# Layer inputs and weights split on other engines, and a ring of four 512-column banks used as two slots of 1024

## What is computed

```python
# layer 0: one head of K0 = 32 channels, then a batch norm over all batches
q, k, v = Wq x + bq, Wk x + bk, Wv x + bv
x = batch_norm(gamma * (v softmax(q k)^T) + x)
# layer 1: group norm (32 groups), one head of 256 channels
q, k, v = split(qkv_w group_norm(x) + qkv_b)
x = x + proj_w (softmax(q k / 16) v) + proj_b
# layers 2 and 3: group norm, eight heads of 32 channels
q, k, v = split(qkv_w xn + qkv_b), per head
x = (xn in layer 2, x in layer 3) + proj_w concat(softmax(q k * 32 ** -0.5) v) + proj_b
```

## Time and profile before

| | us |
|---|---|
| median of 3 runs | 1860.53 (1860.29 to 1861.84) |
| the profiled execution | 1861.36 |
| its span, first to last instruction | 1859.6 |
| TensorE busy | 1673.1 (90%) |
| VectorE busy | 1048.1 (56%) |
| GpSimd busy | 1011.9 (54%) |
| ScalarE busy | 925.8 (50%) |
| mean granted TensorE clock | 0.941 |

### The profile page before, as it was taken

How to read it: one execution, slowest core, us unless ns; L and a number is a source line. 1 busy time by engine, 2 the same in 40 slices (tenths; PEclk the granted TensorE clock), 3 DMA queues, 4 the chain that set the end, 5 groups by cost and what they waited for, 6 DMA issues and landing times.

```text
span 1859.6 us, 25009 instructions
## 1 busy us (share of the span) xinstructions
PE 1673.1 (90%) x8222; PEld 1001.1 (54%) x8222; DVE 1048.1 (56%) x1635; ACT 925.8 (50%) x1487; POOL 1011.9 (54%) x402
## 2 busy tenths in 40 slices
PE   3888869999994789999999997999999999999987
PEld 2666747788883444545545544444454454455522
DVE  2445535454542466667567666675576576656611
ACT  2334414343331246665565564665666566556553
POOL 2323221211213148687677775787688678767764
PEclk7889979999997679999999998999999999999997
DMA  3000000000000330330330320303213123033000
GB/s 140 18 18 1 18 1 1 1 1 1 1 1 23 68 69 1 69 69 1 70 69 1 69 63 24 69 1 74 45 25 69 25 69 69 2 92 70 1 23 23
DMA packets 25000, 67.53 MB, mean 36 GB/s; under 512 B 7200, under 2 KB 8992, under 8 KB 24864
## 3 DMA queue, kind: packets, MB, share of 16 engines
q1 hardware_dynamic: 24864, 65.78, 14.5%
HBM read 7.82 MB, written 4.19 MB: 6 GB/s over the span
## 4 chain that ended last, share of the span: by engine, by line
PE 53%; ACT 4%; SPq 3%; issue 3%; DVE 2%; DMA 1%; POOL 1%; POOLq 0%; ACTq 0%; DVEq 0%
PE psA L952 15%; PE psO L871 12%; PE psD L927 12%; PE psD L79 10%; PE psO L874 4%; ACT PR L1127 3%; SPq L1213 2%; DVE BNS L1004 2%; SPq L1215 2%; DMA QS<-SL 1%; POOL PA L1193 1%; ACT XH L1071 0%; DMA QS<-MROW 0%; PE psD L922 0%; POOL SL L1173 0%
## 5 line engine op out<-in xcount | busy, mean ns | idle before, releaser
L1127 ACT ACTIVATE PR<-psA 128x512 f32<-128x512 f32 x1024 | 582.2, 597 | 480.8 <-PE psA L952 438.1
L1004 DVE TENSOR_REDUCE BNS<-psD 128x1 f32<-128x512 f32 x1024 | 633.5, 683 | 233.8 <-PE psD L927 233.7
L1193 POOL TENSOR_TENSOR PA<-PA,PR 128x2048 f32<-128x2048 f32 x128 | 585.6, 4575 | 16.4 <-ACT PR L1127 4.0
L952 PE MATMUL psA<-QS,KS 97*128 97x512 f32 x1024 | 461.1, 459 | 41.5 <-ACT PR L1127 33.6
L927 PE MATMUL psD<-KS,QS 96*128 96x512 f32 x1024 | 397.8, 429 | 23.4 <-DVE BNS L1004 11.3
L952 PEld LDWEIGHTS psA<-QS,KS 97*128 97x128 f32 x1024 | 191.4, 191 | 351.0 <-ACT PR L1127 199.2
L594 POOL TENSOR_SCALAR P<-P,RS 128x1024 f32<-128x1024 f32 x64 | 72.1, 1126 | 359.3 <-DVE RS L345 359.3
L871 PE MATMUL psO<-PR,V 128*32 128x512 f32 x2048 | 261.4, 618 | 0.7 <-ACT PR L1127 0.7
L927 PEld LDWEIGHTS psD<-KS,QS 96*128 96x128 f32 x1024 | 201.4, 197 | 82.0 <-DVE BNS L1004 37.1
L1193 POOL TENSOR_TENSOR PA<-PR 128x2048 f32<-128x2048 f32 x32 | 146.7, 4585 | 126.0 <-ACT PR L1127 126.0
L1173 POOL TENSOR_TENSOR SL<-SL,SH 128x1024 fp32r<-128x1024 f32 x34 | 80.6, 2373 | 155.2 <-ACT SH L1079 155.2
(11 more groups left out here) (131 smaller groups left out, 1845.7 us busy)
## 6 DMA issues: line engine op xcount, KB each, us to landing
KS<-SH SPq DMA_DIRECT2D x128, 128.0 KB, 2.4
QS<-SH SPq DMA_DIRECT2D x128, 128.0 KB, 2.5
KS<-SL SPq DMA_DIRECT2D x64, 128.0 KB, 2.5
QS<-SL SPq DMA_DIRECT2D x64, 128.0 KB, 2.5
X<-x SPq DMA_DIRECT2D x4, 1024.0 KB, 9.0
out<-X SPq DMA_DIRECT2D x4, 1024.0 KB, 4.3
KH<-KL SPq DMA_DIRECT2D x8, 128.0 KB, 2.4
QH<-KL SPq DMA_DIRECT2D x8, 128.0 KB, 2.4
```

Of the source, the lines that this page charges most:

```text
L952: e.matmul(psA[:, s % 2, :], KS[0:STACK + 1, p, q, j * PART:(j + 1) * PART], QS[0:STACK + 1, p, q, h * HALF:(h + 1) * HALF], start=True, s ...
L1004: top = e.tensor_reduce(MXH[:, h, q, tile:tile + 1], full, AX.X, ALU.max)
L1127: e.activation(PR[:, J % 4, (s % QUADH) * HALF:(s % QUADH + 1) * HALF], psA[:, s % 2, :], ACT.Exp, scale=scale).then_inc(exp_done, 1)
L1193: e.tensor_tensor(PA[:, :], PR[:, (J - 1) % 4, :] if j == 1 else PA[:, :], PR[:, J % 4, :], ALU.add).then_inc(sum_done, 1)
```

## The change

- Layers 0 and 1: TensorE's `project` takes its terms in another order (high x high and low x high for both halves, then high x low) and waits for XL only before the last of them. XL is made by VectorE, for all batches of layer 0 and the first of layer 1; GpSimd keeps the others. In layer 1 ScalarE makes XH straight from X by the group norm's factors, beside VectorE's XN. For batch b + 1 of layer 0 VectorE's two XL instructions stand behind tile 4.
- Layer 3's weights: WH is made by ScalarE at step 12 of the phase, WL by GpSimd behind the third addition and XL.
- Layers 2 and 3: the ring is two slots of 1024 columns. A unit writes a whole slot and may start when the one two before it is taken. There are 32 m units per phase, and one each of v, w, K and Q; the output projection has two. MXH and the joining reduce are gone. ScalarE and VectorE take 1024 columns in one instruction.

```diff
@@ -193,15 +194,17 @@
                                     if b == 0:
                                         e.wait_ge(w_low[layer], 1)
                                     e.wait_ge(xh_done, CT * (b + 1))
-                                    e.wait_ge(xl_done, CT * (b + 1))
                                 slot = slot_taken(("k", i, b))
                                 width = PART if L1 else 2 * K0
                                 cols = slice(PART * i, PART * i + width)
-                                for h in range(2):
-                                    mv = slice(h * HALF, (h + 1) * HALF)
-                                    mm = split_products(e, psD[0:width, slot, mv],
-                                                        [(ww[:, t, cols], xx[:, t, mv])
-                                                         for ww, xx in ((WH, XH), (WL, XH), (WH, XL)) for t in range(CT)])
+                                for k, (ww, xx) in enumerate(((WH, XH), (WL, XH), (WH, XL))):
+                                    if i == 0 and k == 2:
+                                        e.wait_ge(xl_done, CT * (b + 1))
+                                    for h in range(2):
+                                        mv = slice(h * HALF, (h + 1) * HALF)
+                                        for t in range(CT):
+                                            mm = e.matmul(psD[0:width, slot, mv], ww[:, t, cols], xx[:, t, mv],
+                                                          start=(k == t == 0), stop=(k == 2 and t == CT - 1))
                                 mm.then_inc(unit_full, 1)
 
                             def values(i, b):
...
 
+                            def input_low(b):
+                                for t in range(CT):
+                                    e.wait_ge(xh_done, CT * b + t + 1)
+                                    if L1:
+                                        e.wait_ge(xn_done, CT * b + t + 1)
+                                    src = XN[:, t * N:(t + 1) * N] if L1 else X[:, b, t, :]
+                                    e.tensor_tensor(XL[:, t, :], src, XH[:, t, :].bitcast(F32), ALU.subtract).then_inc(xl_done, 1)
+
                             def normalise(b):
                                 for t in range(CT):
                                     e.tensor_scalar(X[:, b, t, :], X[:, b, t, :], BNF[:, t, 0:1], BNF[:, t, 1:2],
...
+                            input_low(0)
...
+                                    if not L1 and i == 4 and more:
+                                        input_low(b + 1)
...
                         def _(e):
                             def input_high(b):
                                 for t in range(CT):
+                                    if b and t == 0:
+                                        e.wait_ge(unit_full, index["v", 1, b - 1] + 1)
                                     if L1:
-                                        e.wait_ge(xn_done, CT * b + t + 1)
-                                        src = XN[:, t * N:(t + 1) * N]
+                                        e.wait_ge(bn_done, CT * b + t + 1)
+                                        e.activation(XH[:, t, :], X[:, b, t, :], ACT.Identity, scale=SCB[:, t, b, 0:1],
+                                                     bias=SCB[:, t, b, 1:2]).then_inc(xh_done, 1)
                                     else:
                                         e.wait_ge(x_loaded[b], 16)
-                                        src = X[:, b, t, :]
-                                    if b and t == 0:
-                                        e.wait_ge(unit_full, index["v", 1, b - 1] + 1)
-                                    e.activation(XH[:, t, :], src, ACT.Copy).then_inc(xh_done, 1)
+                                        e.activation(XH[:, t, :], X[:, b, t, :], ACT.Copy).then_inc(xh_done, 1)
 
...
-        HALVES_AT = {"v": (0, 1), "w": (3.5, 5), "K": (28, 29.3), "Q": (30.6, 31.9), "p": (14.5, 17.5, 20.5, 23.5)}
-        BANKS = 4
+        UNITS_AT = {"v": (0,), "w": (3,), "K": (28,), "Q": (30.6,), "p": (14.5, 20.5)}
+        SLOTS = 2
 
...
-            halves = dict(HALVES_AT)
+            times = dict(UNITS_AT)
             if g == 0 and first:
-                halves |= {"s": (0, 0), "k": (0.5, 0.5), "q": (0.6, 0.6), "v": (1, 1), "w": (2, 2)}
+                times |= {"s": (0, 0), "k": (0.5,), "q": (0.6,), "v": (1,), "w": (2,)}
             if g == 1:
-                halves["s"] = (2.4, 2.4)
+                times["s"] = (2.4, 2.4)
             if g == 0 or first:
-                del halves["p"]
-            units = [(u, at, i) for u, ats in halves.items() for i, at in enumerate(ats)]
-            n = QUADH * NT * 2
+                del times["p"]
+            units = [(u, at, i) for u, ats in times.items() for i, at in enumerate(ats)]
+            n = QUADH * NT
             spacing = (M_AT[1] - M_AT[0] - sum(b - a for a, b in HOLES[g])) / n
             for i in range(n):
...
-        def bank(place, k):
-
-            i = (BASE["all"][place] + k) % BANKS
-            return psD[:, i // 2, i % 2 * HALF:(i % 2 + 1) * HALF]
+        def slot(place, k):
+
+            return psD[:, (BASE["all"][place] + k) % SLOTS, :]
...
-                        full = bank(place, k)
-                        if place or k >= BANKS:
-                            all_taken(place, r, k - BANKS + 1)
+                        full = slot(place, k)
+                        if place or k >= SLOTS:
+                            all_taken(place, r, k - SLOTS + 1)
...
-                            mm = project(full, 2 * PART * gg + PART * (u in "qQ"), i)
+                            mm = project(full, 2 * PART * gg + PART * (u in "qQ"))
                         elif u == "v":
-                            mm = project(full, 2 * C + PART * g, i)
+                            mm = project(full, 2 * C + PART * g)
                         elif u == "w":
-                            halves_v = [j for j, (name, _, _) in enumerate(UNITS[place]) if name == "v"]
-                            all_taken(place, r, halves_v[i] + 1)
-                            for n in range(NT // 2):
-                                st = slice(i * HALF + n * PART, i * HALF + (n + 1) * PART)
+                            all_taken(place, r, [name for name, _, _ in UNITS[place]].index("v") + 1)
+                            for n in range(NT):
+                                st = slice(n * PART, (n + 1) * PART)
                                 mm = e.transpose(full[:, n * PART:(n + 1) * PART], VT[:, st], ident[:, :])
                         elif u == "m":
-                            q, tile, h = i // (2 * NT), i // 2 % NT, i % 2
-                            if i % (2 * NT) == 0:
+                            q, tile = i // NT, i % NT
+                            if tile == 0:
                                 stacks_filled(e, G, [q])
-                            mm = e.matmul(full, QS[0:STACK, g, q, tile * PART:(tile + 1) * PART],
-                                          KS[0:STACK, g, q, h * HALF:(h + 1) * HALF], start=True, stop=True)
+                            for h in range(2):
+                                mv = slice(h * HALF, (h + 1) * HALF)
+                                mm = e.matmul(full[:, mv], QS[0:STACK, g, q, tile * PART:(tile + 1) * PART],
+                                              KS[0:STACK, g, q, mv], start=True, stop=True)
                         elif u == "T":
                             all_taken(place, r, k)
                             mm = e.transpose(full[0:QUADH * NT, 0:PART], MX[:, :], ident[:, :])
...
-                            q, tile, h = i // (2 * NT), i // 2 % NT, i % 2
-                            top = e.tensor_reduce(MXH[:, h, q, tile:tile + 1], full, AX.X, ALU.max)
-                            if i == 2 * QUADH * NT - 1:
-                                e.drain()
-                                top = e.tensor_reduce(MX[:, :].rearrange("p (q t) -> p q t", q=QUADH),
-                                                      MXH.rearrange("p h q t -> p q t h"), AX.X, ALU.max)
-                            top.then_inc(vec_free, 1)
+                            e.tensor_reduce(MX[:, i:i + 1], full, AX.X, ALU.max).then_inc(vec_free, 1)
...
-                    def split_next_weights():
-
-                        e.wait_ge(w3_loaded, 16)
-                        e.wait_ge(d_full, units_full(NGRP // 2 - 1, "v"))
-                        e.tensor_copy(WH[:, :, :], w3_staged).then_inc(w3_high, 1)
-                        e.wait_ge(w3_high, 1)
-                        e.tensor_tensor(WL[:, :, :], w3_staged, WH[:, :, :].bitcast(F32),
-                                        ALU.subtract).then_inc(w3_split, 1)
-
...
+                        if what == "weights":
+                            e.wait_ge(w3_loaded, 16)
+                            e.wait_ge(d_full, units_full(NGRP // 2 - 1, "v"))
```

(10 more changed lines are left out.)

75 lines of the change are left out of this document (39 added, 36 removed).

## The result

The changed kernel takes 1917.06 us (median of 4 runs, 1913.16 to 1918.37), the kernel before 1860.41 (4 runs). The ratio is 1.0303, 95% interval 1.0283 to 1.0323: 57 us slower, where +33 was forecast, inside the range.

The account below looks back on a forecast made before the run. TensorE's program, taken in order, was held to bound the fifteen attention phases. The terms -3.8 - 13 - 5 - 6 + 27 + 10 + 12 + 9 + 3 = +33 us gave 1893 us on the median before, range 1842 to 1922.

Parts of the forecast that it names:

- Part 1: Layer 0's input: TensorE starts once XH is there, not XL; -3.8 us at the start, -13 at three batch transitions.
- Part 2: Layer 1's start: ScalarE makes XH straight from X, so TensorE starts sooner; -5 us (4 to 6).
- Part 3: Layer 3's weights: the wait for the DMA moves to ScalarE, not removed; -6 us (-11 to +2).
- (a): K and Q in the ring: TensorE waits for their slots' eviction; +27 us (10 to 30).
- (b): Maximum units in the ring: each may start only with one unread unit ahead; +10 us (-10 to +30).
- (d): Output projection in the ring: longer pairs cover fewer exponentials, residual ahead of maxima, group-mean units; +9 us (0 to 15).
- (c): V's transposes: w now stands whole in step 3, where TensorE is the bound; +12 us over fifteen phases.
- (e): First phase without attention and tail: slots go round in 1.29 us per unit, last residual ends later; +3 us (-2 to +6).
- hand-over dearer than walked: Rival, chance 0.15: each unit's delay also holds the next score, so (b) to (d) reach their upper ends; 1931 us.
- the forecast's own 1875 to 1912: The main case, chance 0.55: total time of the changed kernel between 1875 and 1912 us.
- The ring is free: Rival, chance 0.15: ring waits fall into time lost anyway, only the input and weights parts count; 1836 us, faster.
- grouping wins: Rival, chance 0.03: VectorE is the bound, so larger maxima, evictions and residuals save fixed cost; 1787 us.

Follow-up runs that it names:

- e2_ring_only: The kernel before with only the ring of two slots; 1942.56 us, ratio 1.0443.
- e3_front_only: The kernel before with only the change's input part for layers 0 and 1, layer 3's weights staying on VectorE; 1828.75 us, ratio 0.9827.
- e1_old_ring: The changed kernel with the ring of four banks of before, keeping the input and weights parts; 1828.33 us, ratio 0.9843.
- e6_w3_at_18: e1_old_ring with ScalarE's copy of layer 3's weights (WH) at step 18 in place of 12; 1817.85 us, ratio 0.978.
- e11_half_maxima: The changed kernel with VectorE's maximum reading only the first 512 of a unit's 1024 columns; 1880.15 us, ratio 1.0119.
- e9_vwp_pairs: e1_old_ring with only the halves of v, w and the output projection next to each other in TensorE's order; ratio 0.9956 to the kernel before.
- e4_pairs: e1_old_ring with both halves of every unit next to each other in TensorE's order, each half handed over singly; 1881.73 us, ratio 1.0105.

## Why the prediction was right, and where it was not

The sign, the side of each part and the range held. Step by step:

- **Part 1 (-3.8 - 13 = -16.8).** Layer 0 is 19.2 us shorter. Right, in mechanism and size. The first matmul came at 10.06, with 10.85 forecast, where 0.8 is the earlier input, which is luck. The three transitions gave 14.2, with 13 forecast, and the projection did run at the upper clock, 2.4 us shorter at the third, as forecast. In the ten other kernels with the same input part layer 0 takes 232.2 to 235.4, so -20 to -23.5 is nearer.
- **Part 2 (-5).** The start is 5.0 us shorter, to the tenth. The layer is 10.4 shorter, and that second half was not in the sum: its granted clock is 0.98 in place of 0.96, and 2% of 310 us is 6. Not all of it is the shorter pause's. `e2_ring_only` keeps the pause and its layer 1 is 3.1 us shorter than before, at 0.97; between 281 and 300 us its granted clock is 1.00 where the kernel before has 0.82. That leaves some 2 us of the 5.4 for the pause, and that it caused them is argued, not tried.
- **Part 3 (-6, between -11 and +2).** The mechanism was right: ScalarE waited 6.68 us for the DMA (6 to 8 forecast), and TensorE stood 6.35 us behind it. The step that was a little too kind is "of the 12 us that this place costs I count half back": between the traces of `e3_front_only` and `e1_old_ring` the phase is 3.7 us shorter, and the medians show nothing of it. `e6_w3_at_18` shows that the place was the fault: 7 us by the trace, 10 by the medians, were to be had.
- **(a) K and Q (+27).** In the even phases mechanism and size held: 2.5 us with 2.8 forecast. The two waits for SL are 0.98 to 1.06 us each, with 1.4 forecast, and make 2.0 of the 2.5; what makes the other 0.5 is open. In an odd phase steps 24 to 40 take 25.06 in place of 23.79, 1.3 with 0.9 forecast, but here size is luck in part: the wait is 0.51, and `e11_half_maxima` gets 1.0 of the 1.3 back by a faster reading of the maxima. 7 x 2.5 + 8 x 1.3 = 28.
- **(b) Maximum units (+10). This step failed.** "Walking the even phase from 1191 with these numbers, five stretches between weighings end 0.5, 0.5, -0.2, 0.2 and -0.3 us later" let VectorE start each stretch with work in hand. Measured, it is idle 1.3 to 1.6 us at the double weighings of the even phases in place of 0.7 to 0.85 (at the upper clock), and catches up nothing: 2.4 us in an even phase, where no output projection stands and 0.7 was taken. In an odd one the same stretches take 21.23 and 14.79 us in G = 5, where before they took 18.86 and 14.04: 3.1, with the output projection in it. (b) and (d) together are 7 x 2.4 + 8 x 3.1 = 42 us, where 10 + 9 stood. In the odd phases the split between (a), (b) and (d) is not sharp, as `e9_vwp_pairs` shows. Without any split, steps 8 to 56 are 4.4 us longer there, where 2.6 (2.9 with the group means) stood, and (a), (b) and (d) are 7 x 4.9 + 8 x 4.4 = 70 in place of 46. More than half of it is VectorE's reading, for `e11_half_maxima` takes 2.4 of those 4.4 back. In the even phases `e4_pairs` puts half of (b) on the pairs' order and half on the whole hand-over.
- **(c) v and w (+12).** From step 56 to step 8 of the next phase it is 1.1 us more after the even phase shown and 1.5 more after the odd one of G = 5, where 0.8 was forecast: 7 x 1.1 + 8 x 1.5 = 20 in sum.
- **(e) First phase and tail (+3).** +5.5 and +0.5. From the first to the last matmul of the maximum units it is 46.1 us there, where before it was 40.6; over 31.5 units that is 1.46 each, with 1.29 forecast.

28 + 42 + 20 = 90, where the change stands 84 us above `e1_old_ring` in these phases. A few stretches stand for all here, and either trace has some at a lower clock; what makes the 6 us is open. The errors of the sum are (b) and (d) +23, (c) +8, (e) +3, the weights +2, (a) +1, and the front -8: +29, and less those 6 us it is, but for rounding, the 24 by which the forecast was short.

So the total came within 24 us partly by luck: the ring cost 29 us more than the 61 summed for it (84 + 5.5 + 0.5 = 90), and the front gave 8 more than its sum, which hides a part of it. Of the rivals, "hand-over dearer than walked" (0.15, 1931) had the right size: 69 us for (b) to (d), measured 62, and the front's larger gain makes 8 of the rest. The result lies between it and the forecast, 5 us outside the forecast's own 1875 to 1912, so it is this rival that came true more than the forecast. "The ring is free" (3 us for it) fell, with some 89 measured, and "grouping wins" fell altogether: VectorE's busy time did fall by 44 us, as that rival says, and nothing came of it. The sentence of the Trainium skill (Perfetto Trace Analysis, Optimizing Scalar/DVE Operations), that where an engine is not saturated but makes others wait, breaking its instructions up may let work be done sooner, is what these traces bear out: a maximum of 1024 columns takes 1.22 us (1.14 back to back) where two of 512 take 1.21, VectorE is busy for 65% of the stage before, and the smaller hand-over is worth 35 us (`e4_pairs` against the change).

Of the signs that I named, the first matmul, the missing waits for XL, the DMA wait and the waits for SL (24 times, at most 1.1 us, ten of them only 0.5 to 0.7) all showed. The phase lengths did not: 74 to 75 us, once 72, and not 71 to 73 for even groups, 80 to 85 and not 79 to 80 for odd ones with output projection (90 with the weights).

## What to carry to other kernels

A ring's depth counts in pieces, not in bytes: two slots of 1024 columns hold as much as four banks of 512, but while the producer is away (here 1.92 us for a weighing) the consumer has one whole piece at most ready, and in these traces the consumer, which read as slowly as it was fed, then never caught up. Join pieces only where the joined instruction is clearly cheaper than its parts; look that up first (1.22 against 1.21 us), and the answer is there. And where an engine's lead is two steps, keep its other work spread between the steps; when work moves to an engine whose queue others wait on, place it behind the time at which its input lands, not merely after its predecessor.
